# Gated linear attention in halves of 64 tokens, zero products on TensorE at the start, and a new instruction order

## The chip, the cores and the metric

The kernel runs on one core of a Trainium2 chip. The metric is the device time of one execution in microseconds (us). A core has five engines that run side by side, each with a queue of its own: TensorE (PE: matrix products, with a weight load before each), VectorE (DVE), ScalarE (ACT), GpSimd (POOL) and SyncE (SP, which here issues every DMA). They meet only in semaphores. PE writes into PSUM, eight banks of 128 partitions by 512 floats, from which DVE and ACT read.

## The reference, cut to what matters

The input is x, 4 sequences of 1024 tokens with 256 features. Three parts follow one another:

```
x = x + 0.5 * ffn(layernorm(x))        # routed feed-forward: 256 -> 1024 -> 256, relu, with a rank-4 term per expert
z = layernorm(x)
h = rmsnorm(z) * ln1;  q, k, v = h @ wq, h @ wk, h @ wv           # 16 heads of 16
i = exp(clip(h @ wi + bi));  f = sigmoid(h @ wf + bf)             # one of each per token and head
C_t = f_t * C_(t-1) + i_t * v_t k_t^T;  n_t = f_t * n_(t-1) + i_t * k_t
y_t = (C_t q_t) / max(|n_t . q_t|, 1)
z = z + y @ wo;  z = z + mlp(rmsnorm(z) * ln2);  x = x + z        # mlp: silu-gated, 256 -> 704 -> 256
x = x + 0.5 * ffn(layernorm(x))
```

The change is in the recurrence. It is computed in chunks of 128 tokens. Inside a chunk, y is a masked product of (k q) with a matrix of decays and with i v. What came before the chunk enters through the state C. The column of ones beside v gives n in the same product, so a head has 17 columns (HV).

## The kernel before, in words

The 4096 tokens are 8 blocks of 512, each of 4 tiles of 128 tokens; a chunk is a tile. Each block goes through runs "1" (first feed-forward), "A" (projections), then the recurrence of its 4 chunks, "L" (the gated mlp) and "2" (second feed-forward). RUNS interleaves them so that one block's recurrence lies between the feed-forward products of others.

On each engine the work is written as several streams (generators); a `yield` ends a step. ORDER is a string per engine, written by a planner, that says which stream takes the next step ("2G 2U" is two steps of G and two of U). All engines are in order, so a step that has to wait holds all that stand behind it. On PE, U is the first product of a run, V the second, G the transposes and the routing product, and the recurrence has three streams: S, M and Y.

Most products of U and V are float32r pairs, three matrix instructions for one product (L1044 to L1046, `product`), each with 128 weight columns and 256 moving columns.

The recurrence of one chunk before the change, in four units of 4 heads (QUAD, NQ):

- SP (stream E) loads the forget gates of 4 heads, 512 numbers broadcast to all partitions (256 KB), into `dm`. DVE scans them into decays (L979, with `ident4` that starts each row on the diagonal).
- PE multiplies keys and queries (S, L1236): 4 products of 128 by 128 in bf16. DVE multiplies by `dm` into `pt` (L990).
- PE multiplies `pt` with the values `vp` (M, L1255): for each head four products with 32 weight columns, one for each strip of 32 columns of the array, 17 moving columns. A float32 product is two matrix records in the trace, so that is 32 records a unit.
- POOL multiplies the values with the last column of the decays (L562, `wv`). PE makes from these the addition to the state (Y, L1282), DVE masks it (L1004, L1007), POOL decays the old state and adds (L576, L581: `cbd`, `cb`).
- After the fourth unit PE adds q times the state of the chunks before to M (the carry, L1269); its state was finished with the chunk before. Then DVE normalizes (L1012 to L1022, `y`), PE transposes (L1289), ACT and DVE split into high and low part (L757, L1026), PE multiplies with wo and DVE adds to z (L1030).

At the start all weights are loaded and split into a high and a low part by ACT and DVE (streams H).

Of the kernel before, what the change touches and what calls it, by code (L numbers as in the profile page):

```python
# [7 lines left out]
P = 128  # L8
N_SEQ, SEQ, D = 4, 1024, 256
TILES = 4  # L10
# [16 lines left out]
NQ = H // QUAD  # L27
UNITS = TILES * NQ
# [37 lines left out]
class Run:  # L66


    def __init__(self, i):
# [19 lines left out]
        2G 2U 2G 3U V 2U V U V U V 4U V 2U V U 2V 2G 6U G 2U 2G U G 7U V 2U V U V U V 3U 2S U V 2U V U V 2S 2M Y V 2S 2M S Y M S M G Y S G 2U S M 2U M 2U S M  # L89
        Y U S G U Y 2M G S Y U S 2M U G U S U M G Y 3U Y U S V M U M U Y V 2M U M V Y U V Y 2U Y U 2S U V 2U V G U V 2S 2M V 2U G 2U V 2U 2S 3M V 2U V G 2S Y  # L90
        2U G Y M V U G U V U S G M Y M V 4U V 2U V U V U V 3U G U V 2U V U G 2V 2U S 2U S M 2U G S Y U M U M Y G M S M Y S 2M G U Y G 2U S 3U S U M U V U M Y
        U V M Y M U M V U V Y 2U Y U S U V 2U V G U V S V 2U G 2U V 2U V S 2U V S M G M Y 2U G V U G U V U G 2S 2M V 4U V 2U V U V U V 3U G U V 2U V U G 2V 2U
        S 2U S Y 2U G 2M U Y 2S 2M U G M Y 2S G Y 2M G U Y U S U S U 2M 2U 2S M Y 2U V Y M U M U Y V 2M U M V Y U V Y 2U Y 2U V 2U V U V G 2S Y V 2U G 2U V 2U
        V 2U V 2S 2M G 2U G S V U G U V U G S 3M V 4U V 2U V U V U V 3U G U V 2U V U G 2V 2U S 2U S Y 2U G 2M U Y 2S 2M U G Y M 2S G M Y M G U Y U S U S 3U 3M
        Y S U S U V M U M Y U V M Y M U M V U V Y 2U Y 2U V 2U V U V G 2S V 2U G 2U V 2U 2S V 2U V 2M Y G 2U G 2S V U G U V U G 2M V 4U V 2U V U V U V 3U G U
        V 2U V U G 2V 2U S 2U S Y 2U G M U M Y S M S U M G M Y 2S G Y 2M G U Y 2U S U M 3U Y S 2M U S Y V M 2U S M Y V M U V 2M Y U V Y 3U S Y U V 2U V U V G
        2S M V 2U G 2U V 2U V 2U V 2S 2M G 2U G S V U G U V U G S 2M V 3U Y U V 2U V U V U V 3U G U V 2U V U G 2V 2U S 2U Y M 2U G S M U Y S M U M Y G M 2S M
        Y G M G 2U S U Y U S 2U 3M Y 2U 2S V M U M Y U V M Y M U M V U V Y 3U S Y U V 2U V U V S G V S 2U G S U M U M V 2U S M V U V U G 2U V 2U G V 2U S V S
        Y M 4U S Y 2M U S M U G S M S M G Y S Y U G Y 2M 2U G U Y S M 3U Y U S 2M V 2U S Y M S M V Y S M U V S 2M Y U V U Y U S U Y S U M V M S 2U M V G S 2M
        S U V Y U S V Y 2M U S Y M U Y G S 2M U V S M Y 2U S M Y V 2U S M V Y S M S M U M Y U V S M Y U 3M U Y V Y V G 4U G U V U V U V U G 2U G V U G U V U G  # L100
        V 4U V 2U V G U V U V G 4U G V 2U V G U V U V 4U V 2U V U V U V 4U V 2U V U 2V""",
    "DVE": """
        H 4G 2H G H G H G 6H G H 2R 4H R 2H R H R G R H R 2H R 4H 2R 6G R 2G 2R G 5R 2G R G 2R G 4R 2D R 2D 2R G R P R P R 2D R 2P Y R G P G Y P G D Y P D G P
        Y D G R G R G P R G R D R G R P D 2R 2Y D G P Y P R D R G R Y P R G R D G 2Y R P D R Y D 2P R 2G D Y D G R 2Y D R Y D R Y R G P G P R D R G 2P R D 2R
        G R G R G R G D 3R G P R P D 2R Y R G Y 2R P R G Y R D R G R D R 3G 2R G P R G Y P D R D 4R G 2R 3G R G 2R G R P 3R Y 2R Y G P Y P D G R Y G 2R P Y G
        Y R D R P D R D R P 2G P R Y 2D Y G Y R D R Y D R Y R G P G R D R G P 3R D 2R G 2R G 2R 2G R G 2R P R G P 2R Y R G R D R G R D R 3G 2R G P R G Y P R D
        R D 3R G 2R 3G R G 2R G 3R Y R 2P R G R Y 2P G 2Y G R Y D 2R P G Y D R P D R D G 2P R D G 2Y R D Y 2P R Y G D R D 2Y R Y R D Y R G D G 2R G 2P R Y 2R
        D 2R G R D 2R G R 2G R G 2R P R P G 3R G D 2R G R D R 3G 2R G P R G Y P R D R D 3R G 2R 3G R G 2R G 3R Y R 2P R G R Y 2P G 2Y G R Y D 2R P G Y D R P D
        R D 2G R 2P 2Y R 2D 2P R Y 2D Y R Y G R Y R Y R G D G D 2R P G P 3R D R G R D 3R G R G R 2G 2R P R P G 2R Y R G D 2R G R D R 3G 2R G P R G Y P R D R D
        3R G 2R 3G R G 2R G 3R Y R 2P R G R Y 2P G 2Y G R Y R D R P R G R Y 2D P R Y P Y R D Y P D R P D Y P 3G D R 2Y D R Y R P Y R G D G D R D R P G P 3R D  # L110
        2R G R D 2R G R 2G R G 2R P R P G 3R G D 2R G 2R 3G 2R G P R G 2Y R D R D 3R G 2R 3G R G 2R G R P 2R Y R P 2R Y G 2P 2Y G D G 2R P R Y G D R P R Y 2D
        R 2P Y R Y 2D 2P R Y 2G D Y R Y G 2D R Y R P Y R G D G R D R P G 2R D R 2G 2R G R G P 3R G P R P D 3R D 2R G 4R 2G 4R G Y G R Y R P R G D R P 2R 2P D
        G Y P Y R G 2Y 2R G R Y D R P G Y D R P Y R 2D Y 2P R D Y P D Y P R 3G 2D 2Y P 2R Y P D Y R G P G 2D P R P G D R P 2Y D Y P 2R D Y P R Y D R P Y R D R
        P Y 2R Y R G D R P 2D 2P Y 2R Y R D R P Y D R P Y D G P 2G R Y 2R Y 2R Y 2G R G 5R G R G 2R 2G R G 3R G 3R G 2R G 2R 2G R G R G R G 2R G 2R G R G R G
        12R""",
    "ACT": """
        G H 2G H 3G H 2G 10H G 2R 4H R 2H R H R H R 2H R 4H R 4G Z G 3Z G 3R G R 2G 5R A R 2G A 3G R A 2R G A 8R Y 6G 9R A R 3G A 3G Y R 2G A 2R A G 2R Y 2R Y
        3R 5G R 4Z R G 5R 2G R 4G 2R 2G Y 3R G 2R 3G R G 3R G 2R G 2R G R G R 2G 5R A R 2G A Y 2G R A 2R A G 3R Y R Y 3R 4G Z R G 3Z R G 6R 6G 2R 2G 3R G 2R
        3G R G 3R G 2R G 2R G 2R 3G Y 5R A R 2G A 2G R Y A 2R G A 2R Y 2R Y 3R 4G R G 4Z R G 6R 6G 2R 2G 3R G 2R 3G R G 3R G 2R G 2R G R G R 2G Y 5R A R 2G A
        2G R Y A 2R G A 3R Y R Y 3R 4G R Z G 3Z R G 6R 6G 2R 2G 3R G 2R 3G R G 3R G 2R G 2R G R G R 2G Y 5R A R 2G A 2G R Y R A R G A 2R Y 2R Y 3R 4G R G 4Z R  # L120
        G 6R 6G 2R 2G 3R G 2R 4G 4R G 2R G 2R G R G R 2G Y 5R A R 2G A 2G Y 2R A R A G 3R Y R Y 4R 5G 4Z R G 5R 3G R 2G 4R G 11R A 2G A 4G Y G R G A 2R Y A G
        3R Y 2R Y 2R 5G Z R 3Z R Y G 2R Y 6R Y 2R Y R 5G 3R G 4R 6G 2R 2G 3R G 2R 4G R G R 2G R G 2R G 9R""",
    "POOL": """
        H 4G A G 3A 4W 2Q 2W Y G 2W G W 2A G 3W 2A 2Y 2W 2Y 4W Y 2W Y 2Q 4G 4W 2Y 3G W A W A 2W 2Y A W A Y 7W 2Q 4G 2W Y 2W 3G 2A 2W 2Y A W A 4W 2Y 3W 2Y 2Q
# [30 lines left out]
def build(nc, a, out):  # L155
# [4 lines left out]
    with ctx:  # L160
# [50 lines left out]
        u_st = sb("u_st", [P, 2, BLOCK], F32R)  # L211
# [19 lines left out]
        vp = sb("vp", [P, 2, TILES, H, HV])  # L231
# [21 lines left out]
        f_d = nc.dram_tensor("f_scratch", (2, TILES, H, P), F32).ap()  # L253
# [4 lines left out]
        s_setup, s_half = sig("setup_done"), sig("half_bias_done")  # L258
        s_x = [[sig(f"x_loaded{n}_{h}") for h in range(2)] for n in range(XBUFS)]
# [1077 lines left out]
```

## Time and profile before

| | |
|---|---|
| time, median of 3 runs | 987.48 us (985.0 to 989.41) |
| profiled execution, its own time | 983.92 us |
| its span, first to last instruction | 982.1 us |
| busy PE, DVE, ACT, POOL | 904.4, 716.5, 353.3, 247.2 us |
| mean granted clock of TensorE | 0.965 of full |

Busy time of PE is the time in which a matrix instruction was in flight; instructions overlap, so the cost of one is read from start to start in the timeline and not from its duration. The granted clock has two levels, 1.2 and 2.4 GHz; 0.5 is the low one, and a value in between is a stretch that had both. An idle time of an engine is put down to the instruction whose signal ended it.

### The profile page before, as it was taken

To read this page: it belongs to the slowest core of one execution; us is meant where nothing else is said; L and a number is where in the kernel's file an instruction comes from. 1 tells how busy PE (TensorE), PEld (TensorE's weight loads), DVE (VectorE), ACT (ScalarE), POOL (GpSimd) and SP (SyncE) were. 2 spreads that over 40 slices of the span, in tenths; PEclk is the share of its full clock that TensorE was granted. 3 is DMA by queue.
4 is the path that set the end of the run, shared out by engine and by line. 5 is a ranking of instruction groups with operands and counts; after the bars stand their busy time and mean duration, and the time that the engine had idled before them with its cause. 6 is when DMAs were issued, how large, how long until landed. Compare 5 with 4: busy or idle time off the path is not lost.

```text
span 982.1 us, 29559 instructions
## 1 busy us (share of the span) xinstructions
PE 904.4 (92%) x12008; PEld 865.6 (88%) x12008; DVE 716.5 (73%) x1516; ACT 353.3 (36%) x692; POOL 247.2 (25%) x285
## 2 busy tenths in 40 slices
PE   3957889999899998999999999999999989997998
PEld 2857889999789997999889997999989978987998
DVE  6634798985857859786787859887688888895642
ACT  5452251433415352343514433252423341313431
POOL 1021252320431123321412304411323143411100
PEclk9877989999999999999999999999999989998999
DMA  8105455220452126330462105531353156510000
GB/s 289 56 16 147 130 148 150 76 74 5 124 139 69 52 61 167 104 85 23 120 172 85 51 24 157 148 90 30 83 161 119 36 161 175 152 46 1 2 21 23
DMA packets 73077, 92.67 MB, mean 94 GB/s; under 512 B 10638, under 2 KB 47246, under 8 KB 72944
## 3 DMA queue, kind: packets, MB, share of 16 engines
q1 hardware_dynamic: 72944, 90.80, 33.0%
q8 instruction: 96, 1.57, 0.7%
q14 instruction: 37, 0.30, 0.1%
HBM read 73.46 MB, written 17.30 MB: 92 GB/s over the span
## 4 chain that ended last, share of the span: by engine, by line
PE 69%; DVE 11%; SPq 8%; issue 6%; DMA 3%; ACT 2%; POOL 1%; DVEq 0%; ACTq 0%; POOLq 0%
PE bank L1044 19%; PE bank L1046 18%; PE bank L1045 18%; SPq L425 5%; PE bank L1079 3%; PE bank L1255 3%; PE bank L1202 2%; PE bank L1236 2%; DMA dm<-f_scratch 2%; DVE dm L979 2%; SPq L443 1%; PE bank L1269 1%; DVE pt L990 1%; PE bank L1282 1%; DVE a_st L892 1%
## 5 line engine op out<-in xcount | busy, mean ns | idle before, releaser
L624 ACT ACTIVATE r_h<-bank 128x512 fp32r<-128x512 f32 x128 | 76.4, 598 | 280.3 <-PE bank L1079 280.2
L979 DVE TENSOR_TENSOR_SCAN dm<-dm,ident 128x512 f32<-128x512 f32 x128 | 159.7, 1254 | 22.9 <-DMA dm<-f_scratch 22.6
L1044 PE MATMUL bank<-wo_hi,r_h 128*128 128x256 f32 x512 | 147.2, 287 | 4.3 <-DVE r_l L807 4.0
L1044 PE MATMUL bank<-xT_hi,wi_hi 128*128 128x256 f32 x512 | 148.6, 290 | 1.9 <-DVE r_l L807 1.5
L1045 PE MATMUL bank<-wo_hi,r_l 128*128 128x256 f32 x512 | 144.5, 282 | 0.0
L1046 PE MATMUL bank<-wo_lo,r_h 128*128 128x256 f32 x512 | 144.4, 282 | 0.0
L1046 PE MATMUL bank<-xT_lo,wi_hi 128*128 128x256 f32 x512 | 144.4, 282 | 0.0
L1045 PE MATMUL bank<-xT_hi,wi_lo 128*128 128x256 f32 x512 | 144.2, 282 | 0.0
L807 DVE SCALAR_TENSOR_TENSOR r_l<-bank,r_h 128x512 fp32r<-128x512 f32 x128 | 87.5, 684 | 77.4 <-ACT r_h L624 76.8
L562 POOL TENSOR_TENSOR wv<-vp,dm 128x68 f32<-128x68 f32 x128 | 49.8, 399 | 245.9 <-DVE dm L979 132.5
L1044 PE MATMUL bank<-xT_hi,wgu_hi 128*128 128x256 f32 x352 | 102.7, 292 | 2.4 <-DVE xT_lo L941 2.1
L1044 PEld LDWEIGHTS bank<-wo_hi,r_h 128*128 128x128 f32 x512 | 97.2, 190 | 5.5 <-issue 5.2
L1044 PEld LDWEIGHTS bank<-xT_hi,wi_hi 128*128 128x128 f32 x512 | 97.7, 191 | 3.8 <-DVE r_l L807 3.3
L1045 PE MATMUL bank<-xT_hi,wgu_lo 128*128 128x256 f32 x352 | 99.6, 283 | 0.0
L1046 PE MATMUL bank<-xT_lo,wgu_hi 128*128 128x256 f32 x352 | 99.4, 282 | 0.0
L1045 PEld LDWEIGHTS bank<-xT_hi,wi_lo 128*128 128x128 f32 x512 | 97.8, 191 | 0.0
L1046 PEld LDWEIGHTS bank<-xT_lo,wi_hi 128*128 128x128 f32 x512 | 97.5, 190 | 0.0
L1046 PEld LDWEIGHTS bank<-wo_lo,r_h 128*128 128x128 f32 x512 | 97.3, 190 | 0.0
L1045 PEld LDWEIGHTS bank<-wo_hi,r_l 128*128 128x128 f32 x512 | 97.2, 190 | 0.0
L990 DVE TENSOR_TENSOR pt<-bank,dm 128x512 f32<-128x512 f32 x128 | 85.7, 681 | 10.4 <-PE bank L1255 9.1
L519 POOL TENSOR_TENSOR g_rs<-g_ve,minus_half 128x4 f32<-128x4 f32 x24 | 29.2, 1216 | 230.4 <-DVE g_ve L920 218.5
L1044 PEld LDWEIGHTS bank<-xT_hi,wgu_hi 128*128 128x128 f32 x352 | 67.5, 192 | 3.6 <-issue 1.7
(158 smaller groups left out, 2198.7 us busy)
## 6 DMA issues: line engine op xcount, KB each, us to landing
dm<-f_scratch SPq DMA_DIRECT2D x128, 256.0 KB, 4.4
arena<-parts_scratch SPq DMA_DIRECT2D x96, 128.0 KB, 3.5
arena<-parts_scratch SPq DMA_DIRECT2D x96, 64.0 KB, 3.7
arena<-parts_scratch SPq DMA_DIRECT2D x32, 192.0 KB, 3.9
x<-in_x SPq DMA_DIRECT2D x16, 256.0 KB, 3.0
parts_scratch<-pa SPq DMA_DIRECT2D x64, 64.0 KB
parts_scratch<-pb SPq DMA_DIRECT2D x64, 64.0 KB
parts_scratch<-pc SPq DMA_DIRECT2D x64, 64.0 KB
```

The costliest lines, as they stand in the source:

```text
L425: sp.dma_start(to, part[:, x % 2, jj * DC * P:(jj + 1) * DC * P]).then_inc(d_parts[x % 2], 16)
L519: nc.gpsimd.tensor_tensor(g_rs[:], g_ve[:], minus_half[:, 0:TILES], ALU.pow).then_inc(g_rstd, 1)
L562: nc.gpsimd.tensor_tensor(wv[:, heads], vp[:, b % 2, j, heads], w, ALU.mult).then_inc(a_wv, 1)
L624: nc.scalar.activation(flat(r_h[:, n]), U[use % 2][:], ACT.Relu).then_inc(f_rh, 1)
L807: v.scalar_tensor_tensor(r_l[:, n].rearrange("p a t -> p (a t)"), U[use % 2][:], 0.0, r_h[:, n].rearrange("p a t -> p (a t)").bitcast(F32) ...
L979: v.tensor_tensor_scan(dm[:, g], dm[:, g], ident4[:], 0.0, ALU.mult, ALU.add).then_inc(a_D, 1)
L990: v.tensor_tensor(pt[:, u % 2], S[u % 2][:], dm[:, u % NQ], ALU.mult).then_inc(a_P, 1)
L1044: nc.tensor.matmul(dst, lh, rh, start=first, stop=False, **more)
L1045: nc.tensor.matmul(dst, ll, rh, start=False, stop=False, **more)
L1046: return nc.tensor.matmul(dst, lh, rl, start=False, stop=last, **more)
L1079: done = nc.tensor.matmul(dst, lora_b[0:LS2, cols], u_st[0:LS2, r.k % 2, h * HALF:(h + 1) * HALF], start=False, stop=True, skip_group_chec ...
L1255: done = nc.tensor.matmul(M[tile, h * HV:(h + 1) * HV], pt[:, u % 2, i * P + q * P // COLS:i * P + (q + 1) * P // COLS], vp[:, b % 2, j, h ...
```

## The change

- Units are 8 heads by half chunks of 64 tokens (GH, NG, TH). A token's decay reaches only inside its half. A chunk has 2 units instead of 4. `dm` has three buffers of one unit (DMBUFS), loaded with both halves at once, and is scanned with `diag`.
- S is now 32 products a unit, each with 32 weight columns and 64 moving columns (its own half of the queries). M is 16 products a unit with 34 moving columns, for the values are laid out as (first half, second half) with zeros in the other half (`vq`, three buffers of two tiles).
- The state is needed at the chunk's middle as well as at its end: `c_at[1]` and `c_at[0]`, made on DVE from the addition in PSUM, and spread over heads by POOL (`c_ex`). The addition (Y) is 8 products with 32 weight columns, and is made for every chunk. The carry (M) is 16 products with 32 weight columns and 68 moving columns (8 in a chunk that opens a sequence), and it now needs this chunk's own addition, not only that of the chunk before.
- `y` and `u_st` have one buffer instead of two. `wo` of the attention is loaded in another order of rows.
- PE has a stream W: 40 steps of 4 bf16 products of zeros, 240 moving columns, into unused columns of bank M, and one before all.
- ACT's first instruction is an activation on a spare column, ahead of its first wait.
- All five orders are new. PE's begins with 12 steps of W; the other 28 lie between the steps of the first hundred and fifty.

```diff
+TH = P // 2
+GH = 8
+NG = H // GH
+UNITS = TILES * NG
+DMBUFS = 3
+VBUFS = 3
+WARM = 40
...
     "PE": """
-        2G 2U 2G 3U V 2U V U V U V 4U V 2U V U 2V 2G 6U G 2U 2G U G 7U V 2U V U V U V 3U 2S U V 2U V U V 2S 2M Y V 2S 2M S Y M S M G Y S G 2U S M 2U M 2U S M
...
+        12W G 3W G W U G U W G U 2W 5U 3V U V 5U V U V U 2V 8W G 2W G U W 2U 2W 3U W G U G U 2W U G U G 4U 2W 3U W 2V 3U Y U 2V 5U S V U W 2V S V 3M 2S 2Y M G
...
# POOL
+                nc.gpsimd.memset(vq[:], 0.0).then_inc(s_zero, 1)
...
+                def spread(n):
+                    pairs = HH // 2
+                    nc.gpsimd.tensor_tensor(c_ex[n][:].rearrange("p c (q d) -> p c q d", q=pairs),
+                                            c_at[n][:].unsqueeze(2).to_broadcast([P, DC, pairs, 2 * HV]),
+                                            headmask[:].rearrange("p (q d) -> p q d", q=pairs).unsqueeze(1).to_broadcast([P, DC, pairs, 2 * HV]),
+                                            ALU.mult).then_inc(a_ex[n], 1)
...
+                    pool.wait_ge(a_at[1], DC * (n + 1))
+                    pool.wait_ge(a_c, n)
+                    spread(1)
...
# ACT
+                act.wait_ge(s_setup, 1)
+                nc.scalar.activation(spare[:], zero[:], ACT.Identity)
...
# DVE
+                    for c in range(DC):
+                        if opens(b, j):
+                            done = v.tensor_scalar(two(c_at[1][:, c]), added[:, c, :, 0], 1.0, None, ALU.mult)
+                        else:
+                            done = v.scalar_tensor_tensor(two(c_at[1][:, c]), two(c_at[0][:, c]), end(c, 0), added[:, c, :, 0],
+                                                          ALU.mult, ALU.add)
+                        done.then_inc(a_at[1], 1)
...
-                    if n > 1:
-                        dve.wait_ge(a_yT, n - 1)
+                    if n:
+                        dve.wait_ge(a_yT, n)
...
# PE, stream S
-                        for i in range(QUAD):
-                            h = place_of(QUAD * g + i)
-                            done = nc.tensor.matmul(S[u % 2][:, i * P:(i + 1) * P], ks[:, j % 2, h], qs[:, j % 2, h], start=True, stop=True)
+                        for i in range(GH):
+                            h = place_of(GH * g + i)
+                            for q in range(COLS):
+                                tile = slice(q * P // COLS, (q + 1) * P // COLS)
+                                own = slice(q // 2 * TH, (q // 2 + 1) * TH)
+                                done = nc.tensor.matmul(S[n % 2][tile, i * TH:(i + 1) * TH], ks[:, j % 2, h, tile], qs[:, j % 2, h, own],
+                                                        start=True, stop=True)
...
# PE, stream M: the carry
+                        pe.wait_ge(a_ex[1], c_n + 1)
+                        pe.wait_ge(a_qc, DC * (b + 1))
+                        if not opens(b, j):
+                            pe.wait_ge(a_ex[0], n_on(*chunks[c_n - 1]))
+                        heads = M[:, 0:H * HV].rearrange("p (h m d) -> p h m d", m=2, d=HV)
+                        for m in range(1 if opens(b, j) else 0, 2):
+                            for c in range(DC):
+                                for q in range(COLS):
+                                    tile = slice(q * P // COLS, (q + 1) * P // COLS)
+                                    t = j * P + m * TH + q % 2 * (P // COLS)
+                                    of = c_ex[m][:, c].rearrange("p (h e d) -> p h e d", e=2, d=HV)[:, :, q // 2]
+                                    done = nc.tensor.matmul(heads[tile, HH // 2 * c:HH // 2 * (c + 1), m], q32[:, b % 2, c, t:t + P // COLS], of,
+                                                            start=False, stop=True, skip_group_check=True)
...
+            def blank_product(first):
+                nc.tensor.matmul(M[:, 2 * P + 16:4 * P], blank[:, 0:1].to_broadcast([P, P]), blank[:, 0:1].to_broadcast([P, 2 * P - 16]),
+                                 start=first, stop=True, skip_group_check=True)
+
+            def W_():
+
+                for _ in range(WARM):
+                    for _ in range(4):
+                        blank_product(False)
+                    yield
```

## Rows read from the trace of the kernel before

**Rows 1.** The page: busy time, and the chain that ended last.

```profile
PE 904.4 (92%) x12008; PEld 865.6 (88%) x12008; DVE 716.5 (73%) x1516; ACT 353.3 (36%) x692; POOL 247.2 (25%) x285
...
PE 69%; DVE 11%; SPq 8%; issue 6%; DMA 3%; ACT 2%; POOL 1%; DVEq 0%; ACTq 0%; POOLq 0%
```

**Rows 2.** The waits of PE: total us, times, longest.

```profile
PE bank L1202 <- ACT xn L702: 11.2, 2, 10.4
...
PE bank L1289 <- DVE y L1022: 4.4, 6, 1.2
```

**Rows 3.** Windows of 25 us: length, busy PE, PEld, DVE, ACT, POOL, granted clock, DMA.

```profile
0.00:25.00 25.00, 7.50 (x100) 6.62 (x100) 16.62 (x39) 12.73 (x23) 3.72 (x7) 0.99 0.89 289
...
75.00:100.00 25.00, 19.52 (x194) 18.87 (x195) 13.47 (x24) 6.03 (x12) 4.04 (x5) 0.78 0.56 150
```

**Rows 4.** Windows of 5 us, PE alone: length, busy, granted clock, DMA.

```profile
25.00:30.00 5.00, 3.66 (x15) 0.50 0.14 36
...
60.00:65.00 5.00, 5.00 (x23) 0.50 0.00 0
...
85.00:90.00 5.00, 5.00 (x40) 0.91 0.28 66
```

**Rows 5.** Timeline of PE at 214 us: start, us, line, shapes; one unit of M.

```profile
213.95 0.28 PE L1046 MATMUL bank<-wao_lo,yT_hi 128*128 128x256 f32 x1
214.16 0.45 PE L1255 MATMUL bank<-vp,pt 128*32 128x17 f32 x32
...
214.75 0.28 PE L1045 MATMUL bank<-wd_hi,r_l 128*128 128x256 f32 x1
```

**Rows 6.** Timeline of PE at 323 us: one routing step.

```profile
322.76 0.28 PE L1045 MATMUL bank<-xT_hi,wgu_lo 128*128 128x256 f32 x1
322.88 0.28 PE L1046 MATMUL bank<-xT_lo,wgu_hi 128*128 128x256 f32 x1
323.09 0.80 PE L1216 MATMUL bank<-route_w,xn 128*32 128x40 f32 x64
...
324.05 0.28 PE L1045 MATMUL bank<-xT_hi,wgu_lo 128*128 128x256 f32 x1
```

**Rows 7.** Timeline of PE at 155 us: one unit of S.

```profile
155.31 0.28 PE L1046 MATMUL bank<-xT_lo,wi_hi 128*128 128x256 f32 x1
155.43 0.40 PE L1236 MATMUL bank<-arena 96*128 96x128 bf16 x4
...
155.84 0.28 PE L1045 MATMUL bank<-wo_hi,r_l 128*128 128x256 f32 x1
```

**Rows 8.** Timeline of PE at 611 us: state, S, M and carry in a row.

```profile
610.03 0.70 PE L1282 MATMUL bank<-wv,k 128*128 128x136 f32 x4
610.57 0.39 PE L1236 MATMUL bank<-arena 96*128 96x128 bf16 x4
610.88 0.45 PE L1255 MATMUL bank<-vp,pt 128*32 128x17 f32 x32
611.26 0.73 PE L1269 MATMUL bank<-cb,q 128*128 128x136 f32 x4
611.74 0.37 PE L1044 MATMUL bank<-xT_hi,wi_hi 128*128 128x256 f32 x1
```

**Rows 9.** Groups by line and form on DVE and POOL: count, busy, mean ns, idle.

```profile
L979 DVE TENSOR_TENSOR_SCAN dm<-dm,ident 128x512 f32<-128x512 f32 x128 | 159.7, 1254 | 22.9 <-DMA dm<-f_scratch 22.6
L990 DVE TENSOR_TENSOR pt<-bank,dm 128x512 f32<-128x512 f32 x128 | 85.7, 681 | 10.4 <-PE bank L1255 9.1 <-PE bank L1236 0.8
...
L581 POOL TENSOR_TENSOR cb<-cm,cbd 128x272 f32<-128x272 f32 x24 | 18.8, 784 | 10.6 <-DVE cm L1007 6.4 <-DVE dm L979 3.4 <-issue 0.8
```

**Rows 10.** Timeline of ACT at 7 us.

```profile
7.02 1.28 ACT L702 ACT_TABLE_LOAD   x1 [7.02 <-DVE g_nb L923]
```

**Rows 11.** Timeline of PE at the last chunk: carry, then the transposes of y.

```profile
884.09 0.73 PE L1269 MATMUL bank<-cb,q 128*128 128x136 f32 x4
...
886.20 0.41 PE L1289 MATMUL bank<-ident,y 128*128 128x128 f32 x2 [0.68 <-DVE y L1022]
```

More of the change, by code:

```diff
@@ L339, in build @@
         upto = lambda b, j: chunks[:b * TILES + j + 1]
-        n_carry = lambda b, j: sum(not opens(*c) for c in upto(b, j))
-        n_state = lambda b, j: sum(not closes(*c) for c in upto(b, j))
-        n_cb = lambda b, j: sum(not closes(*c) and not opens(*c) for c in upto(b, j))
+        n_on = lambda b, j: sum(not closes(*c) for c in upto(b, j))
         def n_ml(l, s):
@@ L354, in a_use, with values @@
             return OF["A", b].use + n
+        def values(b, j):
+            half, jj = divmod(TILES * b + j, 2)
+            return vq[:, half % VBUFS, jj]
         def part_bank(x):
@@ L686, in projections, with input_gates @@
                     act.wait_ge(d_f, 16 * TILES * b)
-                nc.scalar.copy(fTz[:, 1:P], bank(A_F)[:, 1:P]).then_inc(a_fTs, 1)
+                halves = lambda t: t.rearrange("p (m t) -> p m t", m=2)[:, :, 1:TH]
+                nc.scalar.copy(halves(fTz[:]), halves(bank(A_F)[:, 0:P])).then_inc(a_fTs, 1)
                 yield
+                input_gates(b, 1)
+                yield
+            def input_gates(b, h):
+                half = 2 * b + h
+                if half >= VBUFS:
+                    act.wait_ge(a_wv, NG * 2 * (half - VBUFS + 1))
+                    act.wait_ge(a_O, NG * 2 * (half - VBUFS + 1))
+                else:
+                    act.wait_ge(s_zero, 1)
+                for m in range(2):
+                    rows = slice(m * TH, (m + 1) * TH)
+                    nc.scalar.activation(vq[rows, half % VBUFS, :, :, m, HD], g32[rows, 2 * h:2 * h + 2, 0:H], ACT.Exp).then_inc(a_i, 1)
             def G_():
@@ L723, in G_ @@
                             act.wait_ge(s_setup, n_setup)
-                        nc.scalar.copy(u_st[0:LS, r.k % 2], G[0:LS]).then_inc(g_uh, 1)
+                        nc.scalar.copy(u_st[0:LS], G[0:LS]).then_inc(g_uh, 1)
                         yield
@@ L874, in projections @@
                     dve.wait_ge(d_c, 16 * TILES * b)
-                v.tensor_tensor_scan(cum[:], bank(A_F)[:, 0:P], zero[:].to_broadcast([P, P]), 1.0, ALU.mult, ALU.add).then_inc(f_read, 1)
+                for m in range(2):
+                    t = slice(m * TH, (m + 1) * TH)
+                    done = v.tensor_tensor_scan(cum[:, t], bank(A_F)[:, t], zero[:].to_broadcast([P, TH]), 1.0, ALU.mult, ALU.add)
+                done.then_inc(f_read, 1)
                 yield
@@ L1258, in M_ @@
                         done.then_inc(a_O, 1)
                         yield
-                        if g == NQ - 1 and not opens(b, j):
-                            before = chunks[b * TILES + j - 1]
-                            if opens(*before):
-                                pe.wait_ge(a_cm, n_state(*before))
-                            else:
-                                pe.wait_ge(a_cb, n_cb(*before))
-                            pe.wait_ge(a_qc, DC * (b + 1))
-                            t = slice(j * P, (j + 1) * P)
-                            for m in range(DC):
-                                done = nc.tensor.matmul(M[:, m * HH * HV:(m + 1) * HH * HV], q32[:, b % 2, m, t], cb[:, m],
-                                                        start=False, stop=True, skip_group_check=True)
-                            done.then_inc(a_c, 1)
-                            yield
+                        if g < NG - 1:
+                            continue
@@ L1274, in Y_ @@
+                        done.then_inc(a_c, 1)
+                        yield
             def Y_():
```

347 lines of the change are left out of this document (176 added, 171 removed).

## The prediction

> **What bounds the kernel now.** I read the page first: is there one engine that is busy nearly all the time, and does the chain run over it? PE is busy 904.4 of 982.1 us and holds 69% of the chain; DVE follows with 716.5 us [rows 1]. So a microsecond taken from PE's own instructions is worth about one, and a microsecond taken from DVE only what PE waited for it. PE is idle 78 us in all. The waits of PE say where: 11.2 us are the wait for the first normalized tile, of which 10.4 at the very start, and the others are short, such as 4.4 us in six waits for y [rows 2]. The windows add the place. The four of 25 us up to 100 us hold 65.1 us of busy PE, 34.9 us idle (first and last of them in [rows 3]); the 43 us left are spread over 880 us. The windows of 5 us show the granted clock: from 25 to 90 us it falls to the low level after each gap (0.50 at 25 and at 60 us, the first five matrix-busy microseconds after a stall) [rows 4].
>
> **The recurrence on PE, start to start.** A duration of 0.28 us of a product of L1044 to L1046 is not its cost; these start 0.12 us apart [rows 6] (0.117 over twelve of them). So I take the start of the plain product before a unit, that of the second plain one behind it, and subtract two such steps (0.235). A unit of M, 32 records with 32 weight columns: 214.75 - 213.95 - 0.235 = 0.57 us [rows 5]. A routing step, 64 such records with 40 moving columns: 324.05 - 322.88 - 0.235 = 0.93 us [rows 6]. The 32 further records cost 0.36, so 11 ns each, and going over to narrow products and back costs 0.21 us. Note that 17 and 40 moving columns fit one line: at these sizes the record is paid, not its columns. That is the rate on which the whole change stands. A unit of S costs 0.30 us by the same subtraction, 155.84 - 155.31 - 0.235 [rows 7]; two in a row cost a little less each, so I take 0.27. State and carry, four records of 136 columns each, are 0.54 and 0.48 us to the next start [rows 8], of which the state's contains a going over that I have counted with its neighbour: 0.45.
>
> Before: the order has 115 stretches of narrow steps (M and routing), 5120 records: 115 x 0.21 + 5120 x 0.0112 = 81.5 us. S 128 x 0.27 = 34.6, carry 28 x 0.48 = 13.4, state 28 x 0.45 = 12.6. Together 142 us.
>
> After: M 64 x 32 = 2048 records, S 64 x 32 = 2048 (bf16, one record each), carry 28 x 32 + 4 x 16 = 960, state 32 x 16 = 512, routing 1024: 6592. Counting neighbours in the new order gives 116 stretches, for S, M, carry and state now stand in the same narrow form and often side by side. 116 x 0.21 + 6592 x 0.0112 = 98.2 us. The 1472 records of carry and state have 68 moving columns, more than any narrow row. A record of 136 columns takes 0.12 us [rows 8], one of 68 half of it, four strips abreast 15 ns: 4 ns more, 5.9 us. Together 104 us, so **PE does 38 us less**. Bounds: S in 64 columns of bf16 in strips is not in the trace. If the four strips did not overlap, a product would cost half of the 0.05 us that one of 128 columns takes (four in 0.2, from 155.43 to the next start) [rows 7], 27 ns, and 2048 of them 33 us more. On the other side, if a float32 pair of S's size is what costs 11 ns and a bf16 one half, 11 us less. I take 11 ns because two narrow rows of different width agree on it.
>
> The Trainium skill speaks against this rate: the page "TensorE: Matmul & The Clock Gate", Part 1, under "Wait — 56ns, not 53.3ns?", says that matrix instructions never start less than about 25 ns apart, however small. By that rule the 6592 records would cost 165 us and the 5120 of before 128, so the recurrence would gain nothing and lose some 44 us against the sum above. The trace disagrees with it for products in strips: 11 ns a record, in [rows 5, 6]; the sum goes by the trace.
>
> **The zero products and the clock.** A product of 240 columns should take 240/128 x 0.05 = 0.1 us at the high level and 0.2 at the low, so the 161 are 16 to 32 us of PE time. The first 49 lie where PE sat idle for 10.4 us [rows 2], and the rest have 24 us of gaps up to 100 us [rows 3]. If the cover were gone, the 112 later ones would cost 11 us. What they return: the busy time at the low level is half lost, so a window loses busy x (1 - clock). Over the windows of 5 us from 25 to 90 us that is 1.8 at 25, 2.5 at 60, 0.45 at 85 and 10 us for all thirteen [rows 4], and about 1 before 25 us. Not every gap is filled; I take **8 us** (0 to 11).
>
> **The early activation.** The table load of 1.28 us stands at 7.02 us, behind the wait for the first statistics and ahead of the first normalization for which PE waits [rows 10, 2]. It moves under the load of x: **1.3 us**. POOL's new clearing of 3264 numbers a partition ends before the statistics come if it takes under 5 us; at the 784 ns for 272 of an addition [rows 9] it would be 9.4 us and delay the start by 4. I take 0, for a write of zeros reads nothing.
>
> **DVE, POOL, ACT, DMA.** DVE loses 64 scans of 1.254 and 64 products of 0.681 us, 124 us [rows 9], and 28 masks. It gains 120 small operations on 34 or fewer columns for the state, 16 more for the values and 8 for the sums, each under 0.68 us, so under 98. It ends between 610 and 690 us, below PE. That shortens PE's waits for DVE, such as those for y [rows 2]; of the 43 us of scattered idle time I take a sixth, **7 us** (0 to 22). POOL gets at most 124 operations of 272 numbers at 0.784, 97 us on top of 247 even with nothing removed: half idle still. ACT has 24 more small ones. SP issues 64 loads of 256 KB fewer, which shortens its queue; no gain is counted for that apart from the gaps above.
>
> **The longer chain inside a chunk.** The carry waited for a state made one chunk ago. Now it waits for wv, addition (PE 0.3), two small DVE operations (0.4), a spread on POOL (0.78 [rows 9]) and hops: about 2 us. Behind it, y takes 2.1 us from the carry's start to the transposes [rows 11], and with one buffer of y the next normalization must wait for these. What stands behind a waiting carry on PE is everything. In the new order I count the PE work laid in between: 8 of 32 chunks have under 2 us between addition and carry, and in 11 there is under 1.5 us between carry and transposes (3 before). At 0.3 to 0.7 us each this is **7 us more** waiting (0 to 13).
>
> u_st with one buffer costs nothing: an "A" or "L" run lies between nearly all feed-forward runs, and for the last two the first part of U and a V step, 1.4 us each, cover the copy.
>
> **The sum.** 982.1 - 38 - 8 - 1.3 - 7 + 7 = 934.8 us of span. The execution was 1.8 us longer than its span, and the median of three 3.6 us above that execution: 940 us.
>
> **Rivals.**
> - More than that: the orders were drawn by a planner that may also close idle time, since DVE has 100 us of new room. If PE's 43 us of scattered idle fall by half, 22 us instead of the net 0, the time is about 918; with a bf16 record at half price, 908. For it: idle at PE is mostly DVE's lateness. Against: the chain above. Chance 0.17.
> - S does not overlap in strips: 33 us back, 973. Against it speak both narrow rows; for it, that neither is bf16 nor 64 columns wide. The skill's page "TensorEngine Tiling (Array Packing)", Restrictions, says that column tiling switches the fast weight load off, which S had in its old form; no row here shows that load by itself. Chance 0.10.
> - The zero products don't do what they are for: they fall beside the gaps and delay real work by 11 us, and the clock returns nothing (8): 959. For it: 28 steps are placed by the times that the planner expected. Chance 0.12.
> - Slower: the chain addition, DVE, POOL, carry, DVE, transposes is exposed in most chunks. It is 4.1 us long; it decides against the change when PE stands 47/32 = 1.5 us more in each chunk. At 2 us, 64 us, 1004. For it: three engines in order, each with other work queued ahead. Against: the order puts over 2 us of work in most gaps, and DVE has become lighter. Chance 0.09.
> - My forecast, 920 to 957: 0.52.
>
> **Numbers.** 0.5% is 4.9 us, about what three runs of this kernel can tell from no change. Below 982.5 lie the forecast, the gains, nearly all of the two middle rivals and a third of the last: faster 0.90, same 0.04, slower 0.06. The range from 906 to 973 leaves out the chain's rival and the tail of the gains.
>
> **What would show it.** PE busy near 904 - 38 - 8 + 16 for zeros = 874. S in strips of 32: 32 records in about 0.35 us, start to start, and M the same with 34 columns. Carry about 0.48. The clock at 1.0 in most windows up to 90 us. No table load at 7 us, the first transposes near 9. DVE near 640. Waits of the carry's line for POOL's spread and of the transposes for y under 20 us together. The prediction is wrong if S's records start over 15 ns apart, or if those waits reach 40 us.

## The result, and the profile after

The changed kernel takes 1030.47 us (median of 4 runs, 1025.98 to 1035.77), the kernel before 986.91 us beside it: a ratio of 1.044 [1.039, 1.050]. The forecast was 940 us with a range up to 973, so the time is 57 us beyond the range and on the other side of no change. One execution of a later experiment (one of four with outer dimension sixteen, 1380.24 us at a granted clock of 0.555) was slow as a whole and is left out of its median and ratio.

The page of the kernel after, its busy row and the first row of the chain that ended last:

```profile
PE 902.9 (88%) x12905; PEld 856.8 (83%) x12905; DVE 633.5 (62%) x1503; ACT 358.9 (35%) x717; POOL 243.4 (24%) x234
...
PE 34%; DMA 9%; issue 7%; SPq 5%; DVE 3%; ACT 1%; POOL 1%; ACTq 0%; POOLq 0%; DVEq 0%
```

Against [rows 1], DVE is 83 us lighter, as forecast (633.5, predicted 640), and PE is busy for as long as before, though 22.0 us of it are zero products. But PE is now idle for 126 of 1028.9 us. The chain's shares can't be set beside those of [rows 1]: they are shares of the whole span, and this chain is followed back only to 407.8 us, so its row adds up to 60% and that of before to 100%. Within it DMA has 9 parts of 60, where it had 3 of 100. So the reading goes to the waits. First PE's (total us, times, longest):

```profile
PE bank L1296 <- DMA arena<-parts_scratch: 23.4, 7, 6.2
PE bank L1099 <- DVE r_l L842: 17.2, 8, 7.2
PE bank L1099 <- DVE yT_lo L1080: 11.0, 8, 3.1
PE bank L1099 <- DVE gm L906: 9.4, 7, 6.1
...
PE bank L1360 <- DVE y L1076: 8.0, 6, 1.8
...
PE bank L1351 <- POOL wv L580: 2.0, 1, 2.0
```

The waits that the prediction watched, for y and for POOL, are small. What PE waits for is DVE's ordinary work (r_l, yT_lo, gm), from an engine that is only 62% busy, and the stacks that DMA brings for S (`arena`). Why is a lighter DVE late? Its own waits:

```profile
DVE r_l L842 <- ACT r_h L649: 84.3, 67, 4.0
DVE dm L1019 <- DMA dm<-f_scratch: 62.6, 20, 7.5
```

The wait for the decays' load was 22.6 us before [rows 9]; with half as many loads it is 62.6. One case in full, DVE, PE and SP's queue in the timeline around 640 us, one fence for each:

```profile
635.79 1.22 DVE L1019 TENSOR_TENSOR_SCAN dm<-dm,diag 128x512 f32<-128x512 f32 x1
...
637.35 0.43 DVE L1089 BATCH_NORM_STATS2 z_st<-z 128x6 f32<-128x256 f32 x1
645.27 1.22 DVE L1019 TENSOR_TENSOR_SCAN dm<-dm,diag 128x512 f32<-128x512 f32 x1 [7.49 <-DMA dm<-f_scratch]
646.41 0.67 DVE L842 SCALAR_TENSOR_TENSOR r_l<-bank,r_h 128x512 fp32r<-128x512 f32 x1
```

```profile
639.52 0.40 PE L1134 MATMUL bank<-u_st,lora_b 98*128 98x256 f32 x2
647.13 0.58 PE L1099 MATMUL bank<-xT_hi,wi_hi 128*128 128x256 f32 x1 [7.21 <-DVE r_l L842]
647.51 0.41 PE L1100 MATMUL bank<-xT_hi,wi_lo 128*128 128x256 f32 x1
647.73 0.41 PE L1101 MATMUL bank<-xT_lo,wi_hi 128*128 128x256 f32 x1
```

```profile
635.87 0.54 SPq L508 DMA_DIRECT2D dm<-f_scratch  x1
```

SP issues the load at 635.87, and it ends DVE's wait at 645.27, 9.4 us later. DVE is in order, so r_l, which needed nothing from that load, stood behind the scan, and PE stood 7.21 us for r_l. Then PE's products start 0.22 us apart instead of 0.12, at the low clock (0.50 granted from 645 to 648 us): the stall is paid a second time.

What the load itself does is seen where it moves alone. Windows of 1 us (length, busy PE, PEld, DVE, ACT, POOL, granted clock, DMA share of 16 engines, GB/s), kernel after, a load issued at 584.07, with no other load or store of SP's queue in flight:

```profile
585.00:586.00 1.00, 1.00 (x10) 1.00 (x10) 0.16 (x1) 0.60 (x1) 0.00 (x0) 1.00 0.09 33
586.00:587.00 1.00, 1.00 (x11) 1.00 (x10) 1.00 (x2) 0.00 (x0) 0.00 (x0) 1.00 0.13 49
587.00:588.00 1.00, 1.00 (x11) 1.00 (x11) 0.66 (x1) 0.00 (x0) 0.00 (x0) 1.00 0.14 53
588.00:589.00 1.00, 1.00 (x11) 1.00 (x10) 0.00 (x0) 0.00 (x0) 0.00 (x0) 1.00 0.13 49
589.00:590.00 1.00, 1.00 (x11) 1.00 (x10) 0.00 (x0) 0.40 (x1) 0.00 (x0) 1.00 0.14 53
590.00:591.00 1.00, 1.00 (x11) 1.00 (x9) 0.77 (x4) 0.20 (x1) 0.00 (x0) 1.00 0.06 25
```

And the same 256 KB in the kernel before, a load that was alone at 219 us:

```profile
219.00:220.00 1.00, 1.00 (x11) 1.00 (x10) 0.50 (x1) 0.00 (x0) 1.00 (x1) 1.00 0.05 12
220.00:221.00 1.00, 1.00 (x11) 1.00 (x10) 0.90 (x4) 0.64 (x2) 0.04 (x1) 1.00 0.58 176
221.00:222.00 1.00, 1.00 (x11) 1.00 (x10) 1.00 (x3) 1.00 (x3) 0.00 (x0) 1.00 0.23 74
```

Before, the bytes go in some 2 us (12 + 176 + 74 = 262 KB). After, they trickle at about 51 GB/s with 0.13 of the DMA engines busy, which is 2 of 16, and need some 5 us (33 + 49 + 53 + 49 + 53 + 25 = 262 KB). Loads close together have those two engines between them: two issued at 520.66 and 523.02 ended DVE's waits at 529.33 and 538.94, 8.7 and 15.9 us after their issue. The form of the load tells why:

```diff
-sp.dma_start(dm[:, g], f_d[...].rearrange("h t -> (h t)").partition_broadcast(P))          # outermost dimension 128
+sp.dma_start(dm[:, n % DMBUFS], src.unsqueeze(1).to_broadcast([2, TH, GH * TH]))            # outermost dimension 2
```

The Trainium skill states this rule, on the page "DMA: Bandwidth & Descriptors", under "Why a DMA increments its semaphore by 16 and not by 1" and again in "Rules for kernel authors": the number of DMA engines of a transfer is the largest up to 16 that divides the slowest dimension of both access patterns, and a leading broadcast of c copies confines it to at most c engines. By that rule this load gets 2; the trace agrees (0.13). The first of these sections sends a narrow transfer from a queue like SP's to the lowest-numbered engines. If so, the shares of other transfers there would queue behind it. No row shows an engine's number, but the other transfers are late in fact: x lands 5.8 us after issue at the median, 3.3 in the kernel of the next section, where only this load is changed.

### The profile page after: what moved, and what is told of

Read it like the earlier page. It is cut to its first block, busy times and chain, and to the rows that moved or that the text cites. A ratio compares the mean times of both kernels' runs of the same rounds, so it can differ in the third digit from the quotient of the medians.

```text
span 1028.9 us, 31060 instructions
## 1 busy us (share of the span) xinstructions
PE 902.9 (88%) x12905; PEld 856.8 (83%) x12905; DVE 633.5 (62%) x1503; ACT 358.9 (35%) x717; POOL 243.4 (24%) x234
## 4 chain that ended last, share of the span: by engine, by line
PE 34%; DMA 9%; issue 7%; SPq 5%; DVE 3%; ACT 1%; POOL 1%; ACTq 0%; POOLq 0%; DVEq 0%
PE bank L1099 10%; PE bank L1101 9%; PE bank L1100 9%; DMA dm<-f_scratch 5%; SPq L441 3%; DMA parts_scratch<-pc 2%; PE bank L1134 1%; PE bank L1257 1%; DMA arena<-parts_scratch 1%; DMA x<-in_x 1%; SPq L459 1%; PE bank L1336 1%; DMA c_scratch<-cum 1%; PE bank L1317 1%; SPq L493 1%
## 5 line engine op out<-in xcount | busy, mean ns | idle before, releaser
L1099 PE MATMUL bank<-xT_hi,wi_hi 128*128 128x256 f32 x512 | 150.9, 295 | 13.8 <-DVE r_l L842 13.4
L1099 PE MATMUL bank<-wo_hi,r_h 128*128 128x256 f32 x512 | 149.4, 292 | 3.9 <-DVE r_l L842 3.8
L1019 DVE TENSOR_TENSOR_SCAN dm<-dm,diag 128x512 f32<-128x512 f32 x64 | 81.7, 1280 | 62.8 <-DMA dm<-f_scratch 62.6
L1099 PEld LDWEIGHTS bank<-xT_hi,wi_hi 128*128 128x128 f32 x512 | 99.5, 194 | 16.2 <-DVE r_l L842 14.3
L1099 PE MATMUL bank<-xT_hi,wgu_hi 128*128 128x256 f32 x352 | 103.5, 294 | 10.4 <-DVE gm L865 6.3
L580 POOL TENSOR_TENSOR wv<-vq,dm 128x272 f32<-128x272 f32 x64 | 42.5, 667 | 212.0 <-issue 118.4
L538 POOL TENSOR_TENSOR g_rs<-g_ve,minus_half 128x4 f32<-128x4 f32 x24 | 24.7, 1030 | 207.7 <-DVE g_ve L962 144.0
L587 POOL TENSOR_TENSOR c_ex<-c_at,headmask 128x272 f32<-128x272 f32 x60 | 44.9, 749 | 110.0 <-DVE c_at L1049 60.8
```

The lines of the kernel that those rows point to most:

```text
L538: nc.gpsimd.tensor_tensor(g_rs[:], g_ve[:], minus_half[:, 0:TILES], ALU.pow).then_inc(g_rstd, 1)
L580: nc.gpsimd.tensor_tensor(wv[:, heads].rearrange("p h m d -> p h (m d)"), values(b, j)[:, heads].rearrange("p h m d -> p h (m d)"), w, ALU ...
L587: nc.gpsimd.tensor_tensor(c_ex[n][:].rearrange("p c (q d) -> p c q d", q=pairs), c_at[n][:].unsqueeze(2).to_broadcast([P, DC, pairs, 2 * HV]),
L1019: v.tensor_tensor_scan(dm[:, n % DMBUFS], dm[:, n % DMBUFS], diag[:], 0.0, ALU.mult, ALU.add).then_inc(a_D, 1)
L1099: nc.tensor.matmul(dst, lh, rh, start=first, stop=False, **more)
```

## The experiments

Theory A: the form of the one load costs the time, and without it the sum of the prediction holds. Rivals: B, the zero products delay real work; C, the longer chain and the new order cost it; D, SP's queue does. The kernel before was timed again with each of three groups of experiments (986.68, 986.24 and 985.68 us); ratios are to it.

### The load over many engines, and the zero products taken out

```diff
-sp.dma_start(dm[:, n % DMBUFS], src.unsqueeze(1).to_broadcast([2, TH, GH * TH])).then_inc(d_fb[n % DMBUFS], 16)
+for m in range(2):
+    sp.dma_start(dm[m * TH:(m + 1) * TH, n % DMBUFS], src[m:m + 1].to_broadcast([TH, GH * TH])).then_inc(d_fb[n % DMBUFS], 16)
...    # the waits for these loads count 32 a load instead of 16
```

> The changed kernel with each load of dm as two transfers of 64 partitions instead of one with an outer dimension of two. Theory A (the load is narrow: in the changed kernel a lone load moves about 51 GB/s at 0.13 of the 16 DMA engines and lands after 6.0 to 7.6 us, where the one of before took 3.0 at best and 4.4 in the middle): it lands in about 4.4 us, DVE's idle time for dm falls from 62.6 us to under 30, and the time from 1030 to between 1000 and 1015 us. Theory B (the new orders ask for loads too late or keep SP behind stores, whatever a load takes): DVE still waits over 45 us for dm, PE still about 23 us for the stacks of keys, and the time stays above 1020 us.

Measured: 941.81 us, ratio 0.956 [0.952, 0.960]. Orders, buffers, zero products and bytes are those of the kernel after. Busy row and DVE's wait for the load:

```profile
PE 877.4 (93%) x12905; PEld 833.6 (89%) x12905; DVE 630.5 (67%) x1503; ACT 358.8 (38%) x717; POOL 243.9 (26%) x234
...
L1020 DVE TENSOR_TENSOR_SCAN dm<-dm,diag 128x512 f32<-128x512 f32 x64 | 79.8, 1250 | 2.5 <-DMA dm<-f_scratch 2.5
```

88.6 us of span are gone: 63.1 of PE's idle time (126.0 to 62.9) and 25.5 of its busy time, as the granted clock rises from 0.949 to 0.984. PE's wait for the stacks falls from 23.4 to 1.4 us, for r_l from 17.2 to 2.8, for yT_lo from 11.0 to 2.1. SP too waits less: for the store of `pc` that must land before the stacks are loaded, 8.8 instead of 39.0 us. The gain is larger than theory A had said (1000 to 1015 us), for the load lands 2.9 us after issue and not the 4.4 that it took, and the other transfers are no longer late. (The 6.0 to 7.6 us in that expectation are no times of this load: the row is that of the two loads of wgu weights, which pass through the same tile `dm`.) SP has more to issue here, not less, so D is not what cost the 89 us, nor is C: order and chain are unchanged. The rest of A is tried from the other side below.

```diff
-WARM = 40
+WARM = 0        # and the W steps out of PE's order, with the wait and the product ahead of it
```

> The changed kernel without the 161 products of zeros, nothing else changed. If they cost what PE's busy rows give them (22 us) and return nothing, 1010 to 1015 us. If they lie in gaps and keep the clock up, 1030 to 1040 us. My prediction's own figures (8 us of clock returned, cover complete) give 1038; the start alone, where the first transposes stood until 12.07 us behind 49 of them, gives 1.7 us back.

Measured: 1035.03 us, ratio 1.050 [1.046, 1.055], beside 1.044 for the kernel after. B falls: the zero products cost nothing that their absence would give back. They seem to return 4.6 us, but the intervals overlap. The same edit on the kernel with the wide load:

> The kernel with the wide loads (942 us) without its 161 products of zeros. In the changed kernel, full of stalls, leaving them out cost 4.6 us; in the kernel before, adding them changed nothing that could be measured. If they return the clock here: 946 to 952 us and a lower mean clock than 0.984. If they only fill gaps: 940 to 944. If they delay the start (the first transposes stand behind 49 of them): 938 to 940.

Measured: 943.51 us, ratio 0.958 [0.954, 0.962], granted clock 0.975 instead of 0.984. The intervals overlap: 1.7 us is all that the zero products return here, and it may be nothing.

### The narrow load and the zero products, each alone on the kernel before

```diff
-sp.dma_start(dm[:, g], f_d[...].rearrange("h t -> (h t)").partition_broadcast(P))
+sp.dma_start(dm[:, g], f_d[...].rearrange("h t -> (h t)").unsqueeze(0).unsqueeze(0).to_broadcast([2, P // 2, QUAD * P]))
```

> The kernel before with its 128 loads of dm written with an outer dimension of two, same bytes. Theory A: each lands 2 to 3 us later, and where DVE's scan stands early in its order the whole engine waits; 1000 us or more, DVE's idle time for dm over 50 us. Theory B: its four buffers are asked for a whole chunk ahead, so the slower load is hidden: 985 to 992 us.

Measured: 1365.91 us, ratio 1.386 [1.382, 1.391], from one access pattern; the bytes and their places are the same. A line of its page, and the longest of PE's waits:

```profile
L979 DVE TENSOR_TENSOR_SCAN dm<-dm,ident 128x512 f32<-128x512 f32 x128 | 159.2, 1243 | 387.6 <-DMA dm<-f_scratch 387.6
```

```profile
PE bank L1044 <- DVE r_l L807: 89.5, 31, 17.9
```

A load over 2 engines at 51 GB/s takes 262 / 51 = 5.1 us of these, and 128 of them 658 us. They come several in a row, so 109 of 128 scans wait, and r_l heads PE's waits again. The kernel after has 64 such loads, 329 us, and suffers less than a quarter as much (89 us against 379).

```diff
+WARM = 40       # W steps at the like places of PE's order of before; blank cleared first on DVE; the activation on the spare column at the head of ACT's stream H
```

> The kernel before with the 40 steps of zero products at the same places among the first steps of its order, and the activation on a spare column at the head of ACT's weight stream. If zero products return the clock in gaps that are there anyway: 975 to 983 us. If they delay what is behind them by what they cost at the high clock (0.1 us each): 990 to 1000 us. If neither: within 3 us of 987.

Measured: 988.17 us, ratio 1.001 [0.998, 1.004]. PE is busy 917.8 us, 13 more than in [rows 1], and the granted clock rises from 0.965 to 0.976: what the clock returns is no more than what the products cost.

### How many engines, or how many transfers

The pair of loads of the first experiment differs in two things from the single one: outer dimension and number. Here the number stays at two and each transfer of the pair has outer dimension 2 again:

```diff
-    sp.dma_start(dm[m * TH:(m + 1) * TH, n % DMBUFS], src[m:m + 1].to_broadcast([TH, GH * TH]))
+    sp.dma_start(dm[m * TH:(m + 1) * TH, n % DMBUFS], src[m].unsqueeze(0).unsqueeze(0).to_broadcast([2, TH // 2, GH * TH]))
```

> The kernel with the wide loads (942 us), each of its two transfers written with an outer dimension of two again (two times 32 partitions). If the outer dimension is what narrows a load: a pair lands after 5 us or more, DVE's idle time for dm is back over 40 us, and the time over 1010 us. If it is that one load was made two: 940 to 946, as before.

Measured: 1049.45 us, ratio 1.065 [1.062, 1.067]; DVE waits 79.4 us in 28 for the loads. Against the first experiment only the outer dimension differs, 2 instead of 64, and that is 107.6 us. Windows of 1 us in which nothing but two such pairs moves, issued at 531.96 and 534.57:

```profile
540.00:541.00 1.00, 0.00 (x0) 0.00 (x0) 0.00 (x0) 0.00 (x0) 0.00 (x0) 1.00 0.13 39
541.00:542.00 1.00, 0.00 (x0) 0.00 (x0) 0.64 (x1) 0.00 (x0) 0.00 (x0) 1.00 0.13 49
```

Several narrow transfers in flight move no more than one, with 0.13 of the engines busy, so they share two between them. So it was not the number that helped. The price of the number, on the kernel before:

```diff
-sp.dma_start(dm[:, g], src.partition_broadcast(P))
+for m in range(2):
+    sp.dma_start(dm[m * P // 2:(m + 1) * P // 2, g], src.partition_broadcast(P // 2))
...    # the waits for these loads count 32 a load instead of 16
```

> The kernel before with each of its 128 loads of dm as two transfers of 64 partitions, as in the kernel with the wide loads, where a load landed after 2.9 us against the 4.4 of before. If part of that kernel's gain came from faster loads and not from the halves: DVE's idle time for dm falls from 22.6 to under 12 us and the time to 975 to 982. If not: 985 to 990. If the 128 further issues of 0.36 us hold up SP: over 990.

Measured: 1021.18 us, ratio 1.036 [1.033, 1.039]. It lands as fast (median 3.2 us, 4.4 before), yet DVE waits 49.8 us in 26. By the medians SP spends 2 x 0.58 us on issuing a load instead of 0.36, 149 us instead of 46 in all, and in the timeline a load is issued 2.4 us after its buffer came free (median) instead of 1.6. So D is a likely cost in this kernel, though no run changes SP's issue time alone. With 64 loads, 128 transfers, SP spends 76 us on them and DVE's wait stays at 2.5.

Then the dose. The gates are stored twice (eight times) in DRAM, so that one transfer has outer dimension 4 (16). Both take eight stores of the gates a block instead of four:

```diff
+FCOPIES = 2      # 8 in the second
-f_d = nc.dram_tensor("f_scratch", (2, TILES, 2, H, TH), F32).ap()
+f_d = nc.dram_tensor("f_scratch", (2, TILES, 2, FCOPIES, H, TH), F32).ap()
...
+sp.dma_start(dm[:, n % DMBUFS], src.unsqueeze(1).to_broadcast([2 * FCOPIES, TH // FCOPIES, GH * TH])).then_inc(d_fb[n % DMBUFS], 16)
```

> The kernel with the mended start (940 us), its loads of dm again one transfer each, but with an outer dimension of four: the gates are stored twice in DRAM (two copies of 64 tokens of each half, 8 stores a block instead of 4), and each copy is broadcast to 32 partitions. A measure of dose. If a load runs on as many DMA engines as its outer dimension has steps (2: a lone load 51 GB/s, landed after 5.7 to 7.6 us), four give about 100 GB/s, and it lands after 3.5 to 4.2 us; DVE waits under 20 us for dm, and the time is 938 to 950 us. If only a contiguous or a single outer dimension is wide, it lands after 5 us or more and the time is over 1000.

> The same with eight copies in DRAM and an outer dimension of sixteen. By the same rule all 16 engines work on it, and it lands in 2.7 to 3 us like the pair of wide transfers, with one issue of about 0.5 us on SP instead of two of 0.58; the stores of the gates grow to 512 KB a block. DVE waits under 8 us for dm. 936 to 942 us if the larger stores are hidden; over 945 if they hold up the loads behind them.

Both stand on the kernel of the section below (939.80 us). Measured: 982.01 us with 4 (ratio 0.996 [0.993, 1.000]) and 947.16 with 16 (0.961 [0.957, 0.966]). DVE's idle time before the scans, with 4 and then with 16:

```profile
L1023 DVE TENSOR_TENSOR_SCAN dm<-dm,diag 128x512 f32<-128x512 f32 x64 | 81.7, 1280 | 29.3 <-DMA dm<-f_scratch 29.3
```

```profile
L1023 DVE TENSOR_TENSOR_SCAN dm<-dm,diag 128x512 f32<-128x512 f32 x64 | 79.7, 1248 | 8.1 <-DMA dm<-f_scratch 8.1
```

With 4 the time misses the 938 to 950 us that were expected by 32 us, and the wait the 20 us by 9. The page gives no landing time for a load of this form. From the timelines (issue to the start of the scan that waited for it, medians): 8.5 us in 20 waits of the kernel after, 6.0 in 14 with outer dimension 4, 3.4 in 4 with 16. These are the crowded loads. A load that is alone, issued at 557.11 with outer dimension 4:

```profile
558.00:559.00 1.00, 1.00 (x11) 1.00 (x10) 0.14 (x1) 0.60 (x1) 0.00 (x0) 1.00 0.15 55
559.00:560.00 1.00, 1.00 (x11) 1.00 (x10) 1.00 (x2) 0.00 (x0) 0.00 (x0) 1.00 0.27 106
560.00:561.00 1.00, 1.00 (x11) 1.00 (x10) 0.69 (x1) 0.00 (x0) 0.00 (x0) 1.00 0.25 94
561.00:562.00 1.00, 1.00 (x11) 1.00 (x10) 0.00 (x0) 0.00 (x0) 0.00 (x0) 1.00 0.02 6
```

0.25 of the engines and 100 GB/s, twice the 0.13 and 51, and all is moved some 4 us after the issue, as the expectation had it for the load. And one with 16, issued at 540.75:

```profile
542.00:543.00 1.00, 1.00 (x11) 1.00 (x10) 0.48 (x1) 0.48 (x1) 0.00 (x0) 1.00 0.70 254
543.00:544.00 1.00, 1.00 (x11) 1.00 (x10) 1.00 (x2) 0.00 (x0) 0.00 (x0) 1.00 0.03 8
```

All 262 KB go in little over 1 us. So outer dimension 2, 4, 16 gives a share of 0.13, 0.25 and 0.70 of the engines, and 1030, 982 and 947 us (the first without the mended start, which made 2 us with overlapping intervals). SP's wait for the store of `pc` goes the same way: 39.0, 29.1 and 10.9 us. The kernels with 4 and 16 issue the same number of transfers, and the one with 16 stores more, so the 35 us between them are the outer dimension's. With 16 the 936 to 942 us that were expected are missed by 5 us. The eight-fold store of the gates is the obvious suspect (packets under 512 B 19358 against 12702 in the first experiment), but it wasn't tried without the load, and stays open.

### The start mended

```diff
 # DVE's order
-2G H 2G 2H G H
+H 4G 2H G H
 # ACT, moved ahead of its streams
-    act.wait_ge(s_setup, 1)
-    nc.scalar.activation(spare[:], zero[:], ACT.Identity)
+act.wait_ge(s_blank, 1)
+nc.scalar.activation(spare[:], blank[:, 0:1], ACT.Identity)
...
```

> The kernel with the wide loads, and the start as my prediction took it to be: DVE clears the blank tile before its first statistics, and ACT's activation on a spare column stands ahead of all streams. The table load then stands near 1 us instead of 8, the first zero product near 1 instead of 5 us, and the first transposes near 9 to 9.5 instead of 12.1 us. If the start is on the path that sets the end: 2.5 to 3 us less, 939. If the loads of weights set the pace from 15 us on: 941 to 943.

It stands on the first experiment's kernel. Measured: 939.80 us, ratio 0.954 [0.951, 0.956]: the fastest of all, though not to be told from 0.956. The start of the kernel after, DVE, ACT and PE in the timeline:

```profile
4.96 0.06 DVE L804 MEMSET blank<- 128x1 uint32 x1
...
5.09 7.14 PE L1372 MATMUL bank<-blank 128*128 128x240 bf16 x49 [5.09 <-DVE blank L804]
...
7.98 1.28 ACT L738 ACT_TABLE_LOAD   x1 [7.98 <-DVE g_nb L965]
...
12.07 0.60 PE L1257 MATMUL bank<-ident,xn 128*128 128x128 f32 x4
```

And with the start mended, PE alone:

```profile
0.92 7.96 PE L1374 MATMUL bank<-blank 128*128 128x240 bf16 x49 [0.92 <-DVE blank L806]
8.72 0.60 PE L1259 MATMUL bank<-ident,xn 128*128 128x128 f32 x4
...
12.84 0.63 PE L1259 MATMUL bank<-ident,xn 128*128 128x128 f32 x4 [2.26 <-DVE xT_lo L985]
```

In the kernel after the blank column is cleared at 4.96 us, behind two steps of normalization, so the 49 products, which start at 5.09, end at 12 us and the first transposes (before, PE stood 10.4 us for them [rows 2]) start without a wait of their own at 12.07: the zero products hold them. Mended, the products start at 0.92 and the transposes at 8.72. Of the 3.35 us, 1.8 are left at 19 us: the next transposes wait 2.26 us instead of 1.29, and the products behind them start at the low clock (0.21 us apart from 14.3 to 16.4 us).

## Why the prediction was wrong

**The step that failed** is "SP issues 64 loads of 256 KB fewer, which shortens its queue; no gain is counted for that apart from the gaps above". The loads were counted and their form was not read; what a load takes was put at its old value without a reason. All 64 that stay have outer dimension 2 and go over 2 of 16 engines. That is 88.7 of the 90.5 us of the miss: 1030.47 against the 941.81 of a kernel in which the form of this load alone differs. None of the rivals was about a transfer, so the range could not hold it. The row that should have warned was ahead of the prediction: 22.9 us of idle DVE behind this very load [rows 9], a wait that already ended last there.

**The rest of the sum holds as a whole**, read from the kernel with the wide load (941.8 us for a forecast of 940, PE busy 877.4 for 874), but in part because terms cancel. One unit of each kind in its timeline, where the working is that of the prediction (start of the plain product before, to the second plain one behind, less 0.235):

```profile
109.02 0.28 PE L1102 MATMUL bank<-wo_lo,r_h 128*128 128x256 f32 x1
109.23 0.42 PE L1297 MATMUL bank<-arena 96*32 96x64 bf16 x32
...
109.80 0.28 PE L1101 MATMUL bank<-wo_hi,r_l 128*128 128x256 f32 x1
...
128.95 0.28 PE L1102 MATMUL bank<-xT_lo,wq_hi 128*128 128x256 f32 x1
129.16 0.69 PE L1337 MATMUL bank<-c_ex,q 128*32 128x68 f32 x32
...
130.00 0.28 PE L1101 MATMUL bank<-xT_hi,wq_lo 128*128 128x256 f32 x1
...
180.44 0.28 PE L1102 MATMUL bank<-xT_lo,wgu_hi 128*128 128x256 f32 x1
180.65 0.45 PE L1352 MATMUL bank<-wv,k 128*32 128x68 f32 x16
...
181.25 0.28 PE L1101 MATMUL bank<-xT_hi,wgu_lo 128*128 128x256 f32 x1
```

- S in strips: 0.545 us for 32 records, (0.545 - 0.21) / 32 = 10.5 ns each. It overlaps, as taken, and the rival of 973 us is out. The 25 ns a record that the prediction had quoted from the Trainium skill ("TensorE: Matmul & The Clock Gate", Part 1, under "Wait — 56ns, not 53.3ns?") from start to start do not hold here for products in strips: 10.5 ns, now for bf16 too. What the prediction made of that figure was also a wrong sum: its 44 us come out only if the 0.21 us of each stretch are counted after the change and not before it. With 25 ns on both sides 1472 more records cost 20 us more than in its own sum, and not 44. M with 34 columns: 0.59 us, (0.59 - 0.21) / 32 = 12 ns a record, for 0.57 forecast.
- Carry and state: (0.815 - 0.21) / 32 = 19 ns and (0.575 - 0.21) / 16 = 23 ns, where 15 was taken; 960 x 4 + 512 x 8 ns is 8 us more. PE's gain is 30 us rather than 38 by these units.
- Zero products: 1.7 to 4.6 us back (943.5 to 941.8, and 1035.0 to 1030.5) instead of 8, both with intervals that overlap, and nothing on the kernel before.
- Early activation: nothing. It is no early one in the kernel after: it stands in ACT's stream H, whose first step comes after three of G in the new order. The text on the change ahead of the prediction misread this ("ACT's first instruction"). It runs at 10.76 us, and the table load stays in the way at 7.98.
- Chain: 7 was taken. The waits at its end are 7.5 us for y in six times, where [rows 2] had 4.4, and 0.4 us for POOL's spread, so the price is a few microseconds at most; the slower rival is out.
- What paid for these: the span of the wide-load kernel is 41.8 us under 982.1, and 30 of PE and 2 of the zero products leave 10, where DVE's relief less the longer chain was taken as 0. DVE's relief is the likely source (its wait for these loads alone is 2.5 us where it was 22.6), but this is a remainder, not a measurement. So the 940 against 941.8 is in part luck.

**Signs.** The forecast named PE's and POOL's waits as what would refute it, and they stayed small while the time went up: a list of such signs is only as wide as the list of steps.

## What to carry to other kernels

Read the access pattern of every transfer that a change touches, and not only its bytes and count: the outermost dimension set how many DMA engines carried it, and one line with 2 there cost 89 us here and 379 us in the kernel before. Two transfers of 64 partitions mended it here. Where one transfer of 128 is possible, as in the kernel before, two of 64 instead cost 3.6%. If an engine that is 62% busy is late with work of its own, look for what it waits on at the head of its queue.

## What the runs showed of the hardware

- A broadcast load of 256 KB moved 51 GB/s at outer dimension 2 and 100 at 4. In its fullest microsecond it moved 254 GB/s at 16 (share 0.70) and 176 at 128 (share 0.58). Several transfers of outer dimension 2 at once moved 39 to 49 GB/s together, at a share of 0.13.
- A transfer that goes over few engines makes others late that have nothing to do with it. At the median, x landed after 5.8 instead of 3.3 us and the stacks of 128 KB after 3.7 instead of 2.7. It depends on what is in flight together: in the kernel before with narrow loads, x stayed at 3.0 us, while the stores of the output took 8.5 instead of 2.6.
- Narrow products in strips cost 10.5 to 12 ns a record up to 64 bf16 or 34 float32 moving columns, and 19 to 23 ns at 68 float32 columns.
- Issuing a load of 128 partitions by one plain broadcast took SP 0.36 us at the median, every other form tried, and each transfer of a pair, 0.51 to 0.59 us.
